# Split-float feed-forward block on one core: start-up order on VectorE and a quartered last accumulation

## What is computed

```python
masked_w = weight * mask[None]                    # 8 x 256 x 256
w_bot = einsum('bg,got->bot', cond_8, masked_w)   # one matrix per batch
x = x + einsum('bnt,bot->bno', x, w_bot) + bias   # layer 0
# layer 1: a shared feed-forward and the two best of 8 experts, H=256, I=1024
mlp(x, g, u, d) = (gelu(x @ g) * (x @ u)) @ d
x = x + sum_k w_k * mlp(x, expert_k) + mlp(x, shared)
```

## Time and profile before

| | us |
|---|---|
| median of 3 runs | 422.52 (422.02 to 422.61) |
| the profiled execution, whole | 422.13 |
| the profiled execution, span of its instructions | 420.0 |
| start-up, to the first layer-0 matmul | 13.07 |
| from the start of the last final step to the end of the span | 5.03 |

### The profile page before, as it was taken

How to read it: one execution, slowest core, us unless ns; L and a number is a source line. 1 busy time by engine, 2 the same in 40 slices (tenths; PEclk the granted TensorE clock), 3 DMA queues, 4 the chain that set the end, 5 groups by cost and what they waited for, 6 DMA issues and landing times.

```text
span 420.0 us, 5319 instructions
## 1 busy us (share of the span) xinstructions
PE 414.6 (99%) x1818; PEld 341.2 (81%) x1818; DVE 189.6 (45%) x299; ACT 184.7 (44%) x306; POOL 140.1 (33%) x86
## 2 busy tenths in 40 slices
PE   8999999999999999999999999999999999999996
PEld 6778888888888888888888888888888888888885
DVE  3668654353445445345335554524434333343334
ACT  6676454463223535445222553535422435444431
POOL 1566545343001354435000344543300054443500
PEclk9999999999999999999999999999999999999999
DMA  7965232322011323223102132332300123210001
GB/s 267 357 202 156 96 113 75 114 71 80 0 59 41 108 80 113 81 70 112 37 0 101 37 112 75 112 81 69 112 0 8 43 75 113 80 34 0 2 0 50
DMA packets 14705, 35.05 MB, mean 83 GB/s; under 512 B 1634, under 2 KB 2914, under 8 KB 14690
## 3 DMA queue, kind: packets, MB, share of 16 engines
q1 hardware_dynamic: 14544, 34.74, 25.9%
q10 hardware_dynamic: 146, 0.13, 0.1%
HBM read 32.77 MB, written 2.10 MB: 83 GB/s over the span
## 4 chain that ended last, share of the span: by engine, by line
PE 96%; DMA 1%; SPq 1%; DVE 1%; issue 0%; DVEq 0%; ACT 0%
PE o_ps L338 30%; PE g_ps L317 21%; PE u_ps L317 21%; PE u_ps L323 10%; PE g_ps L323 10%; PE l_ps L282 1%; DMA l_raw<-l_w 1%; PE l_ps L351 1%; PE l_ps L287 1%; PE l_ps L266 1%; DVE l_first L553 0%; SPq L186 0%; PE g_ps L351 0%; PE l_ps L270 0%; SPq L174 0%
## 5 line engine op out<-in xcount | busy, mean ns | idle before, releaser
L714 POOL TENSOR_TENSOR ex_lo<-raw,ex_hi 128x768 fp32r<-128x768 f32 x64 | 123.3, 1926 | 240.8 <-ACT ex_hi L447 240.8
L438 ACT ACTIVATE gelu<-g_ps 128x512 f32<-128x512 f32 x96 | 57.4, 598 | 175.6 <-PE g_ps L323 175.4
L617 DVE SCALAR_TENSOR_TENSOR u_ps<-gelu,route_cur,u_ps 128x512 f32<-128x512 f32 x64 | 48.4, 755 | 125.4 <-ACT gelu L438 125.4
L622 DVE TENSOR_TENSOR h_lo<-u_ps,h_hi 128x512 fp32r<-128x512 f32 x96 | 66.3, 691 | 31.6 <-ACT h_hi L450 30.5
L450 ACT CAST h_hi<-u_ps 128x512 fp32r<-128x512 f32 x96 | 56.4, 587 | 37.1 <-DVE u_ps L612 18.5
L447 ACT CAST ex_hi<-raw 128x768 fp32r<-128x768 f32 x64 | 52.9, 827 | 0.0
L317 PE MATMUL g_ps<-x_hi,ex_hi 128*128 (+1 forms) x128 | 49.8, 389 | 0.0
L317 PE MATMUL g_ps<-x_hi,ex_lo 128*128 (+1 forms) x128 | 49.8, 389 | 0.0
L317 PE MATMUL u_ps<-x_hi,ex_hi 128*128 (+1 forms) x128 | 49.8, 389 | 0.0
L317 PE MATMUL u_ps<-x_hi,ex_lo 128*128 (+1 forms) x128 | 49.8, 389 | 0.0
L338 PE MATMUL o_ps<-h_hi,ex_hi 128*128 128x512 f32 x122 | 47.5, 389 | 0.0
(11 more groups left out here) (112 smaller groups left out, 556.1 us busy)
## 6 DMA issues: line engine op xcount, KB each, us to landing
raw<-experts SPq DMA_DIRECT2D x64, 384.0 KB, 3.1
raw<-shared SPq DMA_DIRECT2D x8, 384.0 KB, 7.5
l_raw<-l_w SPq DMA_DIRECT2D x8, 256.0 KB, 4.9
x_in<-xT SPq DMA_DIRECT2D x8, 256.0 KB, 3.5
outT<-out_sb SPq DMA_DIRECT2D x4, 256.0 KB, 2.1
outT<-out_sb SPq DMA_DIRECT2D x7, 128.0 KB, 2.0
mask<-l_mask SPq DMA_DIRECT2D x2, 128.5 KB, 5.7
outT<-out_sb ACTq DMA_DIRECT2D x1, 128.0 KB, 2.3
```

The source lines that it names most:

```text
L438: act.activation(gelu[:, s % 2], g_ps[:, s % 2], ACT.Gelu_apprx_tanh).then_inc(gelu_done, 1)
L617: dve.scalar_tensor_tensor(u_ps[:, s % 2], gelu[:, s % 2], route_cur[:, k:k + 1], u_ps[:, s % 2], ALU.mult, ALU.mult).then_inc(h_done, 1)
L622: dve.tensor_tensor(h_lo[:, s % H_SLOTS], u_ps[:, s % 2], h_hi[:, s % H_SLOTS].bitcast(F32), ALU.subtract).then_inc(h_lo_done, 1)
L714: pool.tensor_tensor(lo, raw[:, slot], hi.bitcast(F32), ALU.subtract).then_inc(w_lo_done, 1)
```

## The change

The rests of x are worked out at other places between the mixing passes: half 0 after block 3 and half 1 after block 4. A second list of pieces, `LAST_PIECES`, cuts the last batch's output into four pieces of 256 tokens, in the order (half 0, tokens 0 to 255), (half 1, 0 to 255), (half 1, 256 to 511), (half 0, 256 to 511). `final_down` makes twelve matmuls of 256 columns per step into four regions, the fourth being `u_ps[:, 0, 0:256]`; two waits ahead of the first of these three steps stand at the region that needs them, and one of them is new. `add_final` has four adds of 256 columns, and of the four stores SyncE issues pieces 0 and 2 and ScalarE pieces 1 and 3.

```diff
--- before.py
+++ after.py
@@ -37,6 +37,8 @@
 
 
     OUT_PIECES = [(hh, slice(0, T)) for hh in range(HH - 1)] + [(HH - 1, slice(t, t + T // 2)) for t in (0, T // 2)]
+
+    LAST_PIECES = [(hh, slice(t, t + T // 2)) for hh, t in ((0, 0), (1, 0), (1, T // 2), (0, T // 2))]
 
     TOPPED = B
     ROUTED_SHIFTED = TOPPED + 1
@@ -105,7 +107,7 @@
         u_ps = psum("u_ps", [P, 2, T])
         o_ps = psum("o_ps", [P, HH, T])
         l0_ps = psum("l0_ps", [P, HH, T])
-        FINAL_PS = [l0_ps[:, 0], l0_ps[:, 1, 0:T // 2], g_ps[:, 0, 0:T // 2]]
+        FINAL_PS = [l0_ps[:, 0, 0:T // 2], l0_ps[:, 1, 0:T // 2], g_ps[:, 0, 0:T // 2], u_ps[:, 0, 0:T // 2]]
         l0_acc = l0_ps[:, 0]
         mix_ps = u_ps[:, 1, 0:D]
         idle_ps = g_ps[:, 1]
@@ -206,14 +208,16 @@
                     e = expert_of(b + 1, 0)
                     for j in range(CHUNKS):
                         load_expert(b + 1, j, e)
-                for i, (hh, tokens) in enumerate(OUT_PIECES):
-                    if with_next:
+                if with_next:
+                    for i, (hh, tokens) in enumerate(OUT_PIECES):
                         sp.wait_ge(out_done, len(OUT_PIECES) * b + i + 2)
-                    elif i != 1:
-                        sp.wait_ge(last_out_done, i + 1)
-                    if with_next or i != 1:
                         dst = outT[bass.ds(b, 1), :, hh, tokens].rearrange("a p t -> (a p) t")
                         sp.dma_start(dst, out_sb[:, hh, tokens]).then_inc(stored, 16)
+                else:
+                    for i, (hh, tokens) in enumerate(LAST_PIECES):
+                        if i % 2 == 0:
+                            sp.wait_ge(last_out_done, i + 1)
+                            sp.dma_start(outT[B - 1, :, hh, tokens], out_sb[:, hh, tokens]).then_inc(stored, 16)
 
             sp.sem_inc(stored, 1)
             for g in range(2):
@@ -237,7 +241,7 @@
             with sp.Fori(1, B - 1) as b:
                 batch(b, True)
             batch(B - 1, False)
-            sp.wait_ge(stored, 16 * len(OUT_PIECES) * B + 1)
+            sp.wait_ge(stored, 16 * (len(OUT_PIECES) * (B - 1) + len(LAST_PIECES)) + 1)
 
         @block.tensor
         def _(pe):
@@ -343,9 +347,11 @@
             def final_down(s):
                 w_hi, w_lo = weights(s)
                 pe.wait_ge(h_lo_done, STEPS * (B - 1) + s + 1)
-                if s == STEPS - FINAL:
-                    pe.wait_ge(gelu_done, STEPS * B - 1)
-                for ps, (oh, tokens) in zip(FINAL_PS, OUT_PIECES):
+                for n, (ps, (oh, tokens)) in enumerate(zip(FINAL_PS, LAST_PIECES)):
+                    if s == STEPS - FINAL and n == 2:
+                        pe.wait_ge(gelu_done, STEPS * B - 1)
+                    if s == STEPS - FINAL and n == 3:
+                        pe.wait_ge(h_lo_done, STEPS * B - 1)
                     at = DOWN + oh * P
                     for i, (w, x) in enumerate(((w_hi, h_hi), (w_hi, h_lo), (w_lo, h_hi))):
                         mm = pe.matmul(ps, w[:, at:at + P], x[:, s % H_SLOTS, tokens], start=(s == STEPS - FINAL and i == 0), stop=(s == STEPS - 1 and i == 2))
@@ -495,9 +501,10 @@
             with act.Fori(1, B - 1) as b:
                 batch(b, True)
             batch(B - 1, False)
-            hh, tokens = OUT_PIECES[1]
-            act.wait_ge(last_out_done, 2)
-            act.dma_start(outT[B - 1, :, hh, tokens], out_sb[:, hh, tokens]).then_inc(stored, 16)
+            for i, (hh, tokens) in enumerate(LAST_PIECES):
+                if i % 2 == 1:
+                    act.wait_ge(last_out_done, i + 1)
+                    act.dma_start(outT[B - 1, :, hh, tokens], out_sb[:, hh, tokens]).then_inc(stored, 16)
 
         @block.vector
         def _(dve):
@@ -640,7 +647,7 @@
                     dve.tensor_tensor(out_sb[:, hh], x1[:, at + hh * T:at + (hh + 1) * T], o_ps[:, hh], ALU.add).then_inc(rest_done, 1)
 
             def add_final():
-                for i, (ps, (hh, tokens)) in enumerate(zip(FINAL_PS, OUT_PIECES)):
+                for i, (ps, (hh, tokens)) in enumerate(zip(FINAL_PS, LAST_PIECES)):
                     dve.wait_ge(rest_done, hh + 1)
                     dve.wait_ge(final_done, i + 1)
                     dve.tensor_tensor(out_sb[:, hh, tokens], out_sb[:, hh, tokens], ps, ALU.add).then_inc(last_out_done, 1)
@@ -684,12 +691,12 @@
 
             dve.sem_inc(out_done, 1)
             route_top()
-            for g in range(5):
+            for g in range(4):
                 combine_0(g)
             split_x(0, 0)
-            combine_0(5)
+            combine_0(4)
             split_x(0, 1)
-            for g in range(6, G):
+            for g in range(5, G):
                 combine_0(g)
             for oh in range(HH):
                 apply_mask_0(oh)
```

## The result

Over 20 executions of each kernel the changed one takes 421.89 us (median; 420.85 to 422.41) against 422.61 us before (422.02 to 423.28): 0.72 us less, a ratio of 0.9982 with a 95% interval of 0.9975 to 0.9988. The forecast was 0.83 less, 421.7, with within 0.2% as the likeliest class; 0.18% came.

A forecast was written before the change was run, and what follows sets the result against it. TensorE was taken to bound the kernel, carrying 96% of the chain, with VectorE bounding the start-up. Start-up -0.41 and tail -0.42 gave -0.83 us, from a median of 422.52 to 421.7, range 421.1 to 422.5.

The forecast's parts named there:

- The start-up: VectorE's mixing passes: one rest of x leaves the stretch from block 4 to the mask, 0.41 us gained, bounds 0 and 0.41.
- Block 7's landing: Start-up load: lands 0.13 us before VectorE needs it; a rival had a landing catch the start-up gain, 422.1, chance 0.12.
- the rest of half 0 free: VectorE before block 4: this rest runs inside the idle time, 0.46 us to spare, and costs nothing.
- TensorE's mixing ends around 12.05: Start-up on TensorE: last four mixing matmuls wait for block 7, end no later than 12.47, delay nothing on the path.
- The last three steps: TensorE's final matmuls: twelve short ones per step instead of three long and six short cost +0.08 us.
- The moved and the new wait: Waits on gelu and `h_lo` in the first final step: cost nothing, with over 2 us of cover.
- The slower rival: Last three steps: weight loads bind in a long run of short matmuls, 2.1 us added, 423.8; chance 0.07.
- The last adds: VectorE's final adds: last one ends at 417.11 against 417.28, 0.17 us gained net of TensorE's cost, between 0.12 and 0.21.
- The stores: Last output stores: last one lands 2.05 behind its issue instead of 2.3, adding 0.25 us, bounds 0 and 0.40.
- each quarter finds nearly free engines: Last stores: a quarter's 128 KB take 0.37 us, about the 0.36 until the next quarter comes.
- bytes leave early: Last stores: the first quarter is issued at 416.10, 0.55 us earlier, so less transfer is left behind the last add.

The follow-up runs named there:

- e1: Kernel before with only the new order of the rests of x and the old end; 421.86 us against 422.23, ratio 0.9993.
- e4: Changed kernel with only the rest of half 0 moved, the rest of half 1 staying behind block 5; 421.80 us, ratio 0.9989 to the kernel before.
- after: The profiled execution of the changed kernel, whole change against the kernel before; its span is 420.1 us, 0.1 longer than the one before.
- e3: The whole change again, timed beside the kernel before on the same chip; 421.49 us against 422.23, ratio 0.9981.
- e7: Changed kernel with half 0 stored whole, one 256 KB store from ScalarE behind the last add; 421.69 us, ratio 0.9986 to the kernel before.
- e8: Changed kernel with all four last stores on SyncE's queue; 422.32 us, ratio 1.0000 to the kernel before.
- e11: Changed kernel with last-three-step matmuls cut into two of 128 columns, those steps not summed; one execution, 425.38 us.
- e2: Changed kernel with the old order of the rests of x, only the end changed; 422.22 us against 422.23, ratio 0.9993.
- e5: Changed kernel with both rests of x worked out on GpSimd instead of VectorE; 422.76 us, ratio 1.0004 to the kernel before.
- e6: Changed kernel with half 1 of x loaded behind block 7 and the first mask, its identity matmuls in layer 0; 423.78 us, ratio 1.0042 to the kernel before.

## Why the prediction was right, and where it was off

The bound was read rightly: the stretch from the first gate to the first final matmul, 396.22 to 396.27 in every profile, carries a shift at the start through unchanged, and the terms at the two ends make the difference. The time came out near the forecast in part by luck: the measured interval reaches from 0.5 to 1.1 us less and can't tell 0.83 from the 0.74 that the profiles add up to, nor could it show the smaller misses below. (The range's lower end is off by 0.1: 422.52 less 0.41, 0.40, 0.21 and half of 0.6 is 421.2, not 421.1.)

**The start-up**, forecast -0.41: -0.42 to -0.40 in all profiles with the new order (3.67 or 3.68 against 4.09 or 4.08), by the mechanism given, if one counts from the start of block 4's pass. Block 7's landing, with its 0.13 of cover, never showed: the three last passes take 1.65 to 1.66 together wherever they stand in a row, without a wait. That block 4 itself lands anywhere over 1.6 us from one execution to the next (8.26 to 9.86) I had not reckoned with. I had called the rest of half 0 free because it had 0.46 to spare before block 4; in e1 and e4 the load came before that rest was done, and by the estimate above a quarter to a half of the 0.42 goes. How often that happens is open, since only one execution of each kernel is profiled.

**What failed in this part** is the sentence that TensorE's mixing ends around 12.05 and delays nothing on the path. Behind the start of block 4's pass (8.98) that is 3.07, and the "no later than the old 12.47" is 3.49. Measured were 3.3 to 3.9, and since `l_lo` stands behind the second mask product in VectorE's queue, the late mixing gave back 0.08 to 0.2 us in three of the six profiles that have the new order with mixing unchanged (e1, after, e3, e4, e7, e8). In those three the mixing ends 3.8 to 3.9 us behind the start of block 4's pass (12.35 - 8.46 in e4); in the other three, 3.3 to 3.4 (13.12 - 9.86 in after). TensorE was taken to wait for block 7; in e3, e4 and e7 it had fallen behind some 1 us before block 4. I had looked at what the second half of the weights needs, and not at what stands behind the waiting instruction on its engine.

**The last three steps**, forecast +0.08: +0.11 (4.19 or 4.20 against 4.08 or 4.09). The distance in a long row is 0.12, not the 0.119 averaged from sixes. The moved and the new wait cost nothing. The slower rival, a floor under the distance of matmuls with a load each, didn't bind at 256 columns; e11 shows how near it is.

**The last adds**, forecast -0.17 net of TensorE: the last add ends 0.81 behind the start of the last matmul against 1.02, so -0.21, and net of the 0.11 it is -0.10. That is under my lower bound of 0.12. The lag behind TensorE was at the long end of what I took (the last matmul ends at 417.06, the add starts at 417.17), and TensorE's own cost was larger.

**The stores**, forecast -0.25: the last one lands in 2.1 and not in 2.3, with the start right behind the add, so -0.2. The size was nearly right and the reason was not. That each quarter finds nearly free engines is not so, as the engines move bytes without a gap from 417.4 to 419.0. That bytes leave early is worth 0.06 to 0.1 of it: e7, which sends half 0 last, keeps the rest. Where this rest of the gain comes from is open. What e8 shows is a condition: four issues that follow one another at 0.36 need the second queue, or 0.3 us is lost; in the kernel before no issue was late on its queue.

The sum of the stretches is -0.42 - 0.32 = -0.74, less what a late mixing (0.08 to 0.2) or an early load (0.1 to 0.2) gives back in some executions, and -0.72 was measured. That start and end add is shown by the profiles, not by the times of e1 and e2.

## What to carry to other kernels

When an effect is smaller than the scatter of executions, compare stretches between fixed points of the timeline and not spans: here all but one repeat to 0.05 us or so where the times scatter over 1.5. Count them from an event that the change can't move, a landing and not the start of the instruction that waits for it. For an instruction moved out of a chain, count distances between starts, not lengths: an independent instruction of 0.61 between two dependent ones was worth only 0.41, since it also hid the wait for the result. And before moving work to an idle engine or a load to a later place, go through what it shares (the port of e5) and what queues behind it (the casts of e6).

## What was new about the hardware

- One GpSimd subtraction (128x512) beside one VectorE pass with two SBUF inputs (128x256) made that pass 1.565 us long instead of 0.485.
- Matmuls with a weight load each started 0.112 us apart at 128 columns (e11), 0.12 at 256 and 0.227 at 512. The runs don't separate the load's share in the floor.
- Four DMA issues in a row on SyncE were 0.35, 0.43, 0.45 and 0.45 us long (e8), where two on each of two queues were 0.34 to 0.38 long (after). As the last store, 256 KB landed 2.2 behind its issue (e7) and 128 KB 2.1 (after).
- The load of block 4, issued at 3.66 us in each, landed 4.6 us later in e1 and 6.2 in after, 1.6 us apart.
- The warm-up matmul (128x512) took 0.99 us until some moment between 7.2 and 9.7 us, and 0.58 behind it, while the granted clock stood at 1.00 in the windows view throughout; the runs don't show why.
